# A fused attention and FFN block on one core: the first and the last unit worked by batches, one rope product, a shared set-up, and new orders at both ends

## The chip, the cores and the metric

The kernel runs on one core of one Trainium2 chip. The metric is the device time in microseconds of one launch. Lower is better.

## The reference

The input `x` is 32 sequences of 256 positions of 128 features, all float32. What is computed:

```
h = layernorm(x)
q, k, v, g = h @ Wq.T, h @ Wk.T, h @ Wv.T, h @ Wg.T      # 8 heads of 16
q, k = rope(q), rope(k)                                  # x * cos + rotate_half(x) * sin
kv, ksum, vsum = sum_s k^T v, sum_s k, sum_s v           # linear attention, no softmax
o = (q @ kv * scale + vsum) / (q @ ksum * scale + 256)
o = (o + conv5(v, lepe_w) + lepe_b) * g                  # depthwise, 5 taps along the sequence
x = x + o @ Wo.T
y = fp8(layernorm(x) as bf16 / s_in) @ fp8(W / s_k) * (s_in * s_k)
out = x + bf16(y) + bias
```

`fp8` rounds to e4m3fn.

## The kernel before

A unit is two batches (sequences), which is four tiles of 128 positions, so there are 16 units, `u` from 0 to 15 (`LAST`). Nearly all instructions take a whole unit: 128 partitions by 512 columns. `j` is a batch within its unit. All products run on TensorE into seven banks of PSUM. `p_num` takes two of them, and `bank[0]` to `bank[5]` are the rest.

There is no scheduler. Each of the five engines has one list of steps, written out by hand as calls such as `project_qk(2, 1)`, and it runs them in just that order. Each step waits on semaphores that count finished units (`count(u)` is unit `u`'s count). The units overlap as a software pipeline: while unit t has its first layernorm, unit t-1 has its projections, unit t-2 its attention, unit t-3 its output projection, unit t-4 its FFN. A loop over t covers the middle, and the first units and the last ones are written out.

The way of one unit, step by step:

- `stats1` (VectorE, L680), `var_eps1` (ScalarE), `pow1` (GpSimd, L476: the variance to the power -0.5, and then a small product, L478), `norm1` (ScalarE, L264), `transpose_h` (TensorE, L902), `move_hT` (ScalarE, L275);
- `project_qk` (TensorE, L912, one call for each batch), `rope` (VectorE, two products for each batch, L687 and L689), `add_rope` (GpSimd, L494, the sum of the two), `transpose_q` (L946) and `key_value` (L957) on TensorE, `mask_kv` (VectorE);
- `project_v` (L923), `transpose_v` (L938), and the five taps of the convolution: three on VectorE (`conv_tap`, L703), two on ScalarE, one sum on GpSimd (`sum_outer`);
- `sum_v` (L968) and `attend` (L976) on TensorE, `invert` and `divide` (VectorE, L727), `transpose_t1` (TensorE, L984), `add_lepe` and `gate` (VectorE, L735 and L743; `project_g`, L931, gives the gate), `project_o` (L991), `residual` (VectorE, L749);
- `stats2`, `var_eps2`, `pow2` (L485), `norm2`, `transpose_h2` (L1000), a quantising step (ScalarE, L358), `ffn` (TensorE, L1034), `move_y`, `add_bias`, `final_sum`, `store`.

For unit 15 the FFN part is already worked by batches (`end_norm2`, `end_transpose_h2`, `end_quantise`, `end_ffn`, `end_half`). Everything ahead of it is worked by whole units.

Before the first unit, TensorE transposes all five weight matrices once all of them and the identity are there, VectorE copies them out of PSUM, and `set_up_ffn` on VectorE rounds the FFN weights in 14 small instructions (L597 to L615 and L603), after a conversion of the identity to bf16 (L596). The loads of `x`, of the tables and of the outputs go through SyncE's queue (SP), four of the weights through ScalarE's. Loads of unit 2 and later stand behind all loads of constants on SP.

## Time and profile before

| | us |
|---|---|
| median of 3 runs | 181.34 (181.03 to 181.6) |
| the profiled execution | 181.48 |
| its span, first to last instruction | 179.7 |
| TensorE busy in the span | 160.3 (89%) |
| VectorE busy | 153.7 (86%) |
| GpSimd busy | 132.7 (74%) |
| ScalarE busy | 131.7 (73%) |

The profiled execution took 181.48 us, of which 1.8 us lie outside its span. Busy shares are averages over the whole span. In the middle all engines have more than these, and at both ends less, so each stage has to be read by itself. Durations of matmuls are modelled from their starts, and neighbours overlap a little. The distance from one start to the next is the better price.

### The profile page before, as it was taken

To read this page: it belongs to the slowest core of one execution; us is meant where nothing else is said; L and a number is where in the kernel's file an instruction comes from. 1 tells how busy PE (TensorE), PEld (TensorE's weight loads), DVE (VectorE), ACT (ScalarE), POOL (GpSimd) and SP (SyncE) were. 2 spreads that over 40 slices of the span, in tenths; PEclk is the share of its full clock that TensorE was granted. 3 is DMA by queue.
4 is the path that set the end of the run, shared out by engine and by line. 5 is a ranking of instruction groups with operands and counts; after the bars stand their busy time and mean duration, and the time that the engine had idled before them with its cause. 6 is when DMAs were issued, how large, how long until landed. Compare 5 with 4: busy or idle time off the path is not lost.

```text
span 179.7 us, 3861 instructions
## 1 busy us (share of the span) xinstructions
PE 160.3 (89%) x1125; PEld 138.4 (77%) x1125; DVE 153.7 (86%) x315; ACT 131.7 (73%) x353; POOL 132.7 (74%) x152
## 2 busy tenths in 40 slices
PE   0379979999999999999999999999999999998431
PEld 0258959878898889898989898989889888976210
DVE  0249999999999999999999999989999999999414
ACT  3443864879797979798888888887889586576561
POOL 1227155697989798888889898988899787838770
PEclk9999999999999999999999999999999999999955
DMA  5740000103012030304030303030301200200214
GB/s 144 207 117 0 0 0 7 58 0 92 28 44 74 21 101 3 115 4 119 4 117 0 117 7 117 4 117 0 104 15 57 67 4 1 58 5 0 62 55 117
DMA packets 19094, 9.71 MB, mean 54 GB/s; under 512 B 1536, under 2 KB 18816, under 8 KB 19072
## 3 DMA queue, kind: packets, MB, share of 16 engines
q1 hardware_dynamic: 18496, 9.19, 17.5%
q10 hardware_dynamic: 576, 0.26, 0.5%
q8 instruction: 10, 0.16, 0.4%
q14 instruction: 12, 0.10, 0.2%
HBM read 5.25 MB, written 4.19 MB: 53 GB/s over the span
## 4 chain that ended last, share of the span: by engine, by line
PE 81%; DVE 8%; issue 3%; ACT 3%; DMA 2%; POOL 1%; ACTq 0%; DVEq 0%; POOLq 0%
PE bank L912 16%; PE bank L991 8%; PE p_num L976 8%; PE bank L957 8%; PE p_num L968 8%; PE bank L923 7%; PE bank L931 7%; PE bank L946 4%; PE bank L902 4%; PE bank L984 4%; PE bank L938 4%; PE bank L1034 2%; DMA xs<-_attn_hidden_states_dram 2%; PE bank L1000 2%; DVE st L680 1%
## 5 line engine op out<-in xcount | busy, mean ns | idle before, releaser
L494 POOL TENSOR_TENSOR qk<-rc,rs 128x512 f32<-128x512 f32 x32 | 40.2, 1272 | 10.3 <-DVE rs L689 10.3
L912 PE MATMUL bank<-w_qk,hT 128*128 128x256 f32 x128 | 34.5, 397 | 0.9 <-ACT hT L275 0.9
L703 DVE SCALAR_TENSOR_TENSOR acc<-bank,conv_w,acc 128x510 f32<-128x510 f32 (+1 forms) x48 | 34.5, 719 | 0.1
L327 ACT ACTIVATE h<-x,nmr,rs 128x128 bf16<-128x128 f32 x60 | 24.7, 483 | 7.4 <-POOL nmr L487 7.4
L264 ACT ACTIVATE h<-xs,nmr,rs 128x128 f32<-128x128 f32 x64 | 26.2, 486 | 3.9 <-POOL nmr L478 3.9
L912 PEld LDWEIGHTS bank<-w_qk,hT 128*128 128x128 f32 x128 | 24.0, 199 | 4.8 <-ACT hT L275 1.3
L476 POOL TENSOR_TENSOR rs<-ve,minus_half 128x4 f32<-128x4 f32 x16 | 16.3, 1016 | 12.7 <-ACT ve L255 12.6
L485 POOL TENSOR_TENSOR rs<-ve,minus_half 128x4 f32<-128x4 f32 x16 | 16.3, 1017 | 11.1 <-ACT ve L318 11.0
L687 DVE TENSOR_TENSOR rc<-bank,cos_t 128x512 f32<-128x512 f32 x32 | 21.8, 681 | 3.0 <-PE bank L912 3.0
L505 POOL TENSOR_TENSOR acc<-acc,outer 128x508 f32<-128x508 f32 x16 | 20.3, 1267 | 2.3 <-DVE acc L703 2.3
L923 PEld LDWEIGHTS bank<-w_v,hT 128*128 128x128 f32 x128 | 17.6, 200 | 5.6 <-issue 5.3
L689 DVE TENSOR_TENSOR rs<-bank,sin_t 128x512 f32<-128x512 f32 x32 | 21.8, 681 | 0.0
L510 POOL TENSOR_TENSOR yc<-yb,fb 128x512 bf16<-128x512 bf16 x15 | 17.3, 1152 | 2.1 <-ACT yb L365 2.1
L680 DVE BATCH_NORM_STATS2 st<-xs 128x6 f32<-128x256 f32 x32 | 12.1, 419 | 7.7 <-DMA xs<-_attn_hidden_states_dram 7.7
L517 POOL TENSOR_TENSOR ob<-x,yc 128x512 f32<-128x512 f32 x15 | 17.3, 1156 | 1.2
L991 PE MATMUL bank<-w_o,oT 128*128 128x128 f32 x128 | 17.0, 276 | 1.0 <-DVE oT L743 0.9
L976 PE MATMUL p_num<-kvs,qT 128*128 128x136 f32 x128 | 17.9, 282 | 0.0
L358 ACT ACTIVATE q<-bank,rsc 128x512 fp8e4<-128x512 bf16 x15 | 10.3, 685 | 10.3 <-PE bank L1000 10.3
L923 PE MATMUL bank<-w_v,hT 128*128 128x128 f32 x128 | 17.7, 284 | 0.0
L957 PE MATMUL bank<-v,qk 128*128 128x136 f32 x128 | 17.7, 281 | 0.0
L968 PE MATMUL p_num<-w_v,hsum 128*128 128x272 f32 x64 | 17.3, 393 | 0.0
L991 PEld LDWEIGHTS bank<-w_o,oT 128*128 128x128 f32 x128 | 15.6, 192 | 2.0 <-DVE oT L743 2.0
(83 smaller groups left out, 335.6 us busy)
## 6 DMA issues: line engine op xcount, KB each, us to landing
xs<-_attn_hidden_states_dram SPq DMA_DIRECT2D x16, 256.0 KB, 2.9
out_dram<-ob SPq DMA_DIRECT2D x15, 256.0 KB, 2.6
cos_t<-in_cos_dram SPq DMA_DIRECT2D x1, 256.0 KB, 4.2
sin_t<-in_sin_dram SPq DMA_DIRECT2D x1, 256.0 KB, 4.9
out_dram<-ob SPq DMA_DIRECT2D x2, 128.0 KB, 1.8
mask<-in_mask_dram SPq DMA_DIRECT2D x1, 68.0 KB, 3.7
w_raw<-in_L_attn_Wq_dram ACTq DMA_DIRECT2D x1, 64.0 KB, 2.7
w_raw<-in_L_attn_Wk_dram ACTq DMA_DIRECT2D x1, 64.0 KB, 3.0
```

Source lines behind the costliest of these rows:

```text
L264: last = nc.scalar.activation(h[:, s, t], xs[:, u % NX, t], ACT.Identity, scale=rs1[:, s, t:t + 1], bias=nmr1[:, s, t:t + 1])
L327: last = nc.scalar.activation(h2[:, s, t], x2[:, u % 3, t], ACT.Identity, scale=rs2[:, s, t:t + 1], bias=nmr2[:, s, t:t + 1])
L494: nc.gpsimd.tensor_tensor(qk[:, u % 2, j].rearrange("p q t d -> p t q d"), rc[:, j].rearrange("p a h (q d) -> p (a h) q d", q=2), rs[:, j] ...
L687: nc.vector.tensor_tensor(rc[:, j], p_qk[j], cos_t[:].rearrange("p a (h d) -> p a h d", h=2), ALU.mult)
L689: nc.vector.tensor_tensor(rs[:, j], p_qk[j][:, :, ::-1, :], sin_t[:].rearrange("p a (h d) -> p a h d", h=2), ALU.mult).then_inc(rope_done[ ...
L703: nc.vector.scalar_tensor_tensor(out=part, in0=p_vT[:, :, lo + off:hi + off], scalar=conv_w[:, k:k + 1], in1=part, op0=ALU.mult, op1=ALU.a ...
L912: last = nc.tensor.matmul(p_qk[j][:, a].rearrange("p h d -> p (h d)"), hT[:, u % 3, t * P:(t + 1) * P], w_qk[:].rearrange("p a q d -> p (a ...
L923: last = nc.tensor.matmul(p_v[:, t], hT[:, u % 3, t * P:(t + 1) * P], w_v[:, 0:D], start=True, stop=True)
L957: last = nc.tensor.matmul(p_kv[:, t // TPB], qk_tile(u, 1, t), v[:, u % 3, t], start=(t % TPB == 0), stop=(t % TPB == TPB - 1))
L968: nc.tensor.matmul(p_num[:, TPB * j:TPB * (j + 1), 0:NW], hsum[:, u % 3, j:j + 1].to_broadcast([P, P]), w_v[:].unsqueeze(1).to_broadcast([ ...
L976: last = nc.tensor.matmul(p_num[:, t, 0:NW], qT[:, u % 2, t * P:(t + 1) * P], kvs[:, u % 2, t // TPB], start=False, stop=(t % TPB == TPB - 1))
L991: last = nc.tensor.matmul(p_proj[:, t], oT[:, u % 2, t * P:(t + 1) * P], w_o[:], start=True, stop=True)
```

## The change

Seven things are changed together.

1. The first unit's front (load, `stats1`, `var_eps1`, `pow1`, `norm1`, `transpose_h`, `move_hT`) goes by batches, into two banks.
2. The last unit's `attend`, `invert`, `divide`, `project_g`, `transpose_t1`, `add_lepe`, `gate`, `project_o`, `residual`, `stats2`, `var_eps2` and `pow2` go by batches, with banks of their own for each batch.
3. `rope` is one product of 1024 columns for each batch in place of two of 512: the result of `project_qk` is read twice against one table `turn`, which holds cos and sin. `add_rope` reads both halves of `turned`.
4. The set-up of the FFN is split: six small instructions stay on VectorE, the seven others run on GpSimd (`round_ffn_weights`). The identity is converted on ScalarE.
5. The weights of q and k are transposed apart from the other three, each set with a semaphore of its own. The constants' loads are split into two groups.
6. TensorE begins with 13 matmuls of zeros, 512 columns of bf16 each.
7. The lists of steps at both ends are in new orders (units 0 to 4 and 8 to 15).

```diff
@@ on SyncE
-            load_x(0)
-            sp.dma_start(ident[:], ident_c).then_inc(w_in, 16)
+            for j in range(BPU):
+                half = slice(TPB * j, TPB * (j + 1))
+                sp.dma_start(xs[:, 0, half], x_v[0][:, half]).then_inc(x_first[j], 16)
+            sp.dma_start(ident[:], ident_c).then_inc(wqk_in, 16)
+            sp.dma_start(turn[:], turn_c).then_inc(turn_in, 16)
             sp.dma_start(w_raw[:, 4], wo).then_inc(w_in, 16)
-            for dst, src in ((cos_t[:], cos_c), (sin_t[:], sin_c)):
-                sp.dma_start(dst, src).then_inc(rope_in, 16)
             load_x(1)
@@ on VectorE
-                nc.vector.tensor_tensor(rc[:, j], p_qk[j], cos_t[:].rearrange("p a (h d) -> p a h d", h=2),
-                                        ALU.mult)
-                nc.vector.tensor_tensor(rs[:, j], p_qk[j][:, :, ::-1, :],
-                                        sin_t[:].rearrange("p a (h d) -> p a h d", h=2),
-                                        ALU.mult).then_inc(rope_done[j], 1)
+                nc.vector.tensor_tensor(turned[:, j],
+                                        p_qk[j].rearrange("p a h d -> p a (h d)").unsqueeze(2).to_broadcast(
+                                            [P, TPB, 2, 2 * D]),
+                                        turn[:], ALU.mult).then_inc(rope_done[j], 1)
@@ on GpSimd, a new function
+            def round_ffn_weights():
+                val, e, r, n = (b[:, 0:D] for b in (qv, qe, qr, qn))
+                pool.wait_ge(scales_done, 1)
+                link(nc.gpsimd.tensor_scalar(e, e, 2.0 ** -6, 1.5 * 2.0 ** 20, ALU.max, ALU.mult))
+                link(nc.gpsimd.tensor_tensor(r, val, e, ALU.add))
+                link(nc.gpsimd.tensor_tensor(r, r, e, ALU.subtract))
+                link(nc.gpsimd.tensor_tensor(n, r, r, ALU.mult))
+                link(nc.gpsimd.tensor_scalar(n, n, 448.0 ** 2, 3e38, ALU.is_gt, ALU.mult))
+                link(nc.gpsimd.tensor_scalar(n, n, 3e38, 0.0, ALU.mult, ALU.mult))
+                nc.gpsimd.tensor_tensor(fwq[:], r, n, ALU.add).then_inc(w_ready, 1)
@@ on TensorE
+            def keep_busy(bank_free, times):
+                for _ in range(times):
+                    nc.tensor.matmul(bank_free[:], zero[:, 0:P], zero[:], start=True, stop=True)
...
-            transpose_h(0)
-            project_qk(0, 1)
+            pe.wait_ge(zero_set, 1)
+            keep_busy(p_gT, 13)
+            turn_weights_qk()
+            transpose_h(0, j=0)
+            turn_weights()
+            transpose_h(0, j=1)
```

The prediction speaks of three places in the orders. The first is the start of VectorE's list. `stats1` is `BN_STATS`, `rope` is the product with `rc`, `rs` or `turned`. Before:

```order
L680 BN_STATS st<-xs 128x6 x4
L588 COPY w_qk<-p_num 128x2x64 x2
L590 COPY w_v<-p_num 128x128
L591 COPY w_g<-p_num 128x128
L592 COPY w_o<-p_num 128x128
L687 TENSOR_TENSOR rc<-bank,cos_t 128x512
L689 TENSOR_TENSOR rs<-bank,sin_t 128x512
L687 TENSOR_TENSOR rc<-bank,cos_t 128x512
L689 TENSOR_TENSOR rs<-bank,sin_t 128x512
L680 BN_STATS st<-xs 128x6 x2
L596 CAST identb<-ident 128x128
```

And of the change, where the first `BN_STATS` row is unit 0 and the next two are units 1 and 2:

```order
L693 MEMSET zero 128x256
L803 BN_STATS st<-xs 128x6 x2
L699 COPY w_qk<-p_num 128x2x64 x2
L705 COPY w_v<-p_num 128x128
L709 COPY w_g<-p_num 128x128
L803 BN_STATS st<-xs 128x6 x2
L713 COPY w_o<-p_num 128x128
L803 BN_STATS st<-xs 128x6 x2
L812 TENSOR_TENSOR turned<-bank,turn 128x1024 x2
L717 RECIPROCAL rsc<-sc 128x2
L718 TENSOR_TENSOR ysc<-sc 128x1
```

`stats1(2)` has moved from behind the first unit's rope to ahead of it, and the cast is gone from this engine. The second place is TensorE's end, from `project_g(14)` on (L931 before). `ffn` stands twice in the program, under two branches, of which one runs. Before:

```order
L931 MATMUL bank<-hT,w_g 128x512
L976 MATMUL p_num<-kvs,qT 128x136 x4
L991 MATMUL bank<-w_o,oT 128x128 x4
L1000 MATMUL bank<-identb,h 128x128 x4
L984 MATMUL bank<-ident,t 128x128 x4
L1038 COMPARE_AND_BRANCH
L1034 MATMUL bank<-fwq,q 128x128 x4
```

Of the change, from `key_value(15)` on (L1187 is `attend(15)`, L1206 `project_o`, L1215 `transpose_h2`, L1141 `project_g(15)`):

```order
L1168 MATMUL bank<-v,qk 128x136 x4
L1157 MATMUL bank<-ident,qk 128x128 x4
L1206 MATMUL bank<-w_o,oT 128x128 x4
L1187 MATMUL p_num<-kvs,qT 128x136 x2
L1215 MATMUL bank<-identb,h 128x128 x4
L1187 MATMUL p_num<-kvs,qT 128x136 x2
```

These rows put `project_o(14)` ahead of `attend(15)`, which is cut in two around `transpose_h2(13)`. Then follow the branches of `ffn(13)`, and behind them TensorE's list goes on with unit 15 by batches, up to `transpose_h2(14)`:

```order
L1141 MATMUL bank<-hT,w_g 128x256 x2
L1196 MATMUL bank<-ident,t 128x128 x4
L1206 MATMUL bank<-w_o,oT 128x128 x4
L1215 MATMUL bank<-identb,h 128x128 x4
```

`project_g(15)` has moved ahead of `transpose_t1(15)`, which stood ahead of `ffn(13)` before. The third place is VectorE's end, from `residual(14)` on. Of the change (L889 is `stats2(14)`; the 16-column rows are `invert` of one batch, the 256-column rows `divide`, `add_lepe` and `gate` of one batch):

```order
L879 TENSOR_TENSOR x<-bank,xs 128x512
L844 TENSOR_SCALAR den<-p_num 128x16
L847 RECIPROCAL rden<-den 128x16
L889 BN_STATS st<-x 128x6 x2
L854 TENSOR_TENSOR t<-p_num,rden 128x256
L844 TENSOR_SCALAR den<-p_num 128x16
L847 RECIPROCAL rden<-den 128x16
L854 TENSOR_TENSOR t<-p_num,rden 128x256
L862 TENSOR_TENSOR t<-bank,acc 128x256
L871 TENSOR_TENSOR oT<-bank,t 128x256
L862 TENSOR_TENSOR t<-bank,acc 128x256
L871 TENSOR_TENSOR oT<-bank,t 128x256
```

Before, `invert(15)` and `divide(15)` stood ahead of `residual(14)`, and each step took the whole unit.

## Rows read from the trace of the kernel before

**Rows 1.** Stretches: us from:to, length, busy of each engine (instructions), clock, DMA.

```profile
10.00:15.00 5.00, 4.27 (x12) 3.55 (x13) 1.97 (x5) 2.60 (x10) 1.93 (x3) 1.00 0.26 77
...
45.00:145.00 100.00, 99.94 (x738) 88.86 (x737) 95.74 (x191) 83.90 (x228) 88.16 (x96) 1.00 0.19 55
...
165.00:170.00 5.00, 3.01 (x18) 1.72 (x18) 2.90 (x7) 2.65 (x8) 4.38 (x5) 1.00 0.18 52
170.00:175.00 5.00, 1.21 (x8) 0.69 (x8) 0.98 (x4) 3.12 (x8) 3.08 (x4) 0.50 0.18 52
```

**Rows 2.** The chain that ended last, in its middle: start us, us, what.

```profile
44.84 0.86 PE bank L931 x2
...
50.21 0.89 PE bank L991 x8
...
53.32 0.95 PE p_num L976 x8
...
129.91 0.86 PE bank L931 x2
```

**Rows 3.** Timeline of the start: start us, us, engine, line, what, count.

```profile
4.31 0.76 DVE L680 BATCH_NORM_STATS2 st<-xs 128x6 f32<-128x256 f32 x2 [4.31 <-DMA xs<-_attn_hidden_states_dram]
...
6.73 1.12 PE L887 MATMUL p_num<-ident,w_raw 128*128 128x128 f32 x4 [6.73 <-DMA w_raw<-in_L_attn_Wg_dram]
...
10.73 3.78 PE L912 MATMUL bank<-w_qk,hT 128*128 128x256 f32 x8 [0.93 <-ACT hT L275]
...
12.91 0.69 DVE L687 TENSOR_TENSOR rc<-bank,cos_t 128x512 f32<-128x512 f32 x1 [2.69 <-PE bank L912]
...
14.55 0.69 DVE L687 TENSOR_TENSOR rc<-bank,cos_t 128x512 f32<-128x512 f32 x1 [0.34 <-PE bank L912]
...
15.91 1.27 POOL L494 TENSOR_TENSOR qk<-rc,rs 128x512 f32<-128x512 f32 x1 [0.35 <-DVE rs L689]
...
26.12 0.66 PE L984 MATMUL bank<-ident,t 128*128 128x128 f32 x4 [0.49 <-DVE t L727]
```

**Rows 4.** DMA issues, x(2) in its window 7.0 to 7.3 us: KB, us to landing.

```profile
xs<-_attn_hidden_states_dram SPq DMA_DIRECT2D x1, 256.0 KB, 4.2
...
sin_t<-in_sin_dram SPq DMA_DIRECT2D x1, 256.0 KB, 4.9
...
out_dram<-ob SPq DMA_DIRECT2D x2, 128.0 KB, 1.8
```

**Rows 5.** Groups by line and shape: busy us, mean ns, idle before.

```profile
L687 DVE TENSOR_TENSOR rc<-bank,cos_t 128x512 f32<-128x512 f32 x32 | 21.8, 681 | 3.0 <-PE bank L912 3.0
L476 POOL TENSOR_TENSOR rs<-ve,minus_half 128x4 f32<-128x4 f32 x16 | 16.3, 1016 | 12.7 <-ACT ve L255 12.6
L727 DVE TENSOR_TENSOR t<-p_num,rden 128x512 f32<-128x512 f32 x16 | 10.9, 683 | 0.1
L478 POOL TENSOR_TENSOR nmr<-nm,rs 128x4 f32<-128x4 f32 x16 | 3.2, 199 | 1.3
L656 DVE TENSOR_TENSOR ob<-x,yc 128x256 f32<-128x256 f32 x2 | 0.8, 424 | 0.1
```

**Rows 6.** Timeline of VectorE's set-up for the FFN.

```profile
16.42 0.85 DVE L596 CAST identb<-ident 128x128 bf16<-128x128 f32 x1
...
18.41 0.23 DVE L609 TENSOR_SCALAR qe<-qe 128x128 f32<-128x128 f32 x1
...
20.50 0.15 DVE L603 COPY qe<-ysc 128x1 f32<-128x1 f32 x1
```

**Rows 7.** Timeline of the end.

```profile
160.52 0.39 PE L1034 MATMUL bank<-fwq,q 128*128 128x128 bf16 x4
...
166.90 0.69 DVE L743 TENSOR_TENSOR oT<-bank,t 128x512 f32<-128x512 f32 x1 [0.75 <-DVE t L735]
...
170.89 1.02 POOL L485 TENSOR_TENSOR rs<-ve,minus_half 128x4 f32<-128x4 f32 x1 [1.20 <-ACT ve L318]
...
176.97 0.42 DVE L656 TENSOR_TENSOR ob<-x,yc 128x256 f32<-128x256 f32 x1
```

More of the change, by code:

```diff
@@ L536, in _ @@
             pow2(1)
-            for t in range(6, 15):
+            for t in range(6, 13):
                 add_rope(t - 3, 1)
@@ L808, in _ @@
             conv_tap(3, 2)
-            for t in range(5, 14):
+            stats1(5)
+            add_lepe(2)
+            gate(2)
+            mask_kv(3)
+            rope(4, 1)
+            quantise_if_wide(1, is_small)
+            residual(2)
+            stats2(2)
+            conv_tap(4, 0)
+            rope(4, 0)
+            invert(3)
+            conv_tap(4, 1)
+            divide(3)
+            conv_tap(4, 2)
+            for t in range(6, 11):
                 stats1(t)
@@ L823, in _ @@
                 conv_tap(t - 1, 2)
+            stats1(11)
+            add_lepe(8)
+            gate(8)
+            rope(10, 1)
+            mask_kv(9)
+            quantise_if_wide(7, is_small)
+            residual(8)
+            stats2(8)
+            conv_tap(10, 0)
+            rope(10, 0)
+            invert(9)
+            conv_tap(10, 1)
+            divide(9)
+            stats1(12)
+            conv_tap(10, 2)
+            add_lepe(9)
+            gate(9)
+            mask_kv(10)
+            rope(11, 1)
@@ new lines, in _ @@
+            quantise_if_wide(8, is_small)
+            residual(9)
+            stats2(9)
+            rope(11, 0)
+            conv_tap(11, 0)
+            conv_tap(11, 1)
+            invert(10)
+            divide(10)
+            conv_tap(11, 2)
+            mask_kv(11)
+            stats1(13)
+            rope(12, 1)
+            add_lepe(10)
+            rope(12, 0)
+            gate(10)
+            quantise_if_wide(9, is_small)
+            invert(11)
+            residual(10)
+            divide(11)
@@ L861, in _ @@
+            stats2(13)
+            divide(14)
+            rope(15, 0)
+            add_lepe(14)
             conv_tap(15, 0)
-            stats2(13)
-            add_lepe(14)
+            gate(14)
             conv_tap(15, 1)
@@ new lines, in _ @@
+            project_g(9, (x2_done, count_last(8)))
+            project_v(11, (hT_done, count_first(11)))
+            project_qk(11, 1, (rope_done[1], count(10)))
+            transpose_t1(9, (qT_done, count(9)))
+            transpose_h2(8, (v_done, count(11)))
+            key_value(10, (rope_done[0], count(10)))
+            transpose_v(11, (tap_done[-1], count(10)))
+            ffn(8, is_small, (q8_done, count(8)))
+            transpose_q(10, (t2_done, count_last(9)))
+            project_o(9, (oT_done, count_last(9)))
@@ new lines, in _ @@
+            project_qk(11, 0, (kvs_done, count(10)))
+            sum_v(10, (t1_done, count_last(9)))
+            transpose_h(12, (yb_done, count(8)))
+            attend(10)
+            project_g(10, (x2_done, count_last(9)))
+            project_v(12, (hT_done, count_first(12)))
+            transpose_q(11, (qT_done, count(10)))
+            key_value(11, (rope_done[0], count(11)))
+            project_qk(12, 1, (rope_done[1], count(11)))
+            transpose_t1(10, (qT_done, count(11)))
@@ new lines, in _ @@
+            project_o(12, (oT_done, count_last(12)))
+            transpose_h2(11, (v_done, count(14)))
+            project_qk(14, 0, (kvs_done, count(13)))
+            sum_v(14, (t1_done, count_last(13)))
+            ffn(11, is_small, (q8_done, count(11)))
+            transpose_t1(13, (qT_done, count(13)))
+            project_g(13, (x2_done, count_last(12)))
+            transpose_h(15, (yb_done, count(11)))
+            key_value(14, (rope_done[0], count(14)))
+            transpose_q(14, (t2_done, count_last(13)))
@@ new lines, in _ @@
+            sum_v(15, (t1_done, count_last(14)))
+            key_value(15, (rope_done[0], count(15)))
+            transpose_q(15, (t2_done, count_last(14)))
+            project_o(14, (oT_done, count_last(14)))
+            attend(15, 0)
+            transpose_h2(13, (yb_done, count(12)))
+            attend(15, 1)
+            ffn(13, is_small, (q8_done, count(13)))
+            project_g(15, (tap_done[-1], count(15)), j=0)
+            project_g(15, (rope_done[1], count(15)), j=1)
+            transpose_t1(15, (qT_done, count(15)), j=0)
```

809 lines of the change are left out of this document (471 added, 338 removed).

## The prediction

> **What bounds the kernel now.** I read the stretches first, then the chain, then the timelines of the two ends. In the 100 us of the middle TensorE is busy 99.94 us, VectorE 95.74, GpSimd 88.16 and ScalarE 83.90, at a granted clock of 1.00 [rows 1]. The chain runs through TensorE's instructions back to back: one `project_g` starts at 44.84 and the one nine units later at 129.91 [rows 2], so a unit costs (129.91 - 44.84) / 9 = 9.45 us of TensorE, and nothing else matters there. The change takes no real product away from TensorE. So the middle keeps its length, unless another engine passes TensorE. Per unit VectorE has 95.74% x 9.45 = 9.05 us of work, 0.40 us under the bound.
>
> Sixteen units at 9.45 are 151 us of a span of 179.7. The other 28 to 29 us lie at the two ends, where TensorE waits or is slow, and there all of the change's effect must come from.
>
> The start: x is there at 4.31, the weights' transposes begin only at 6.73, `project_qk(0)` runs from 10.73 for 3.78 us, rope begins at 12.91, the second `add_rope` at 15.91, and the first `transpose_t1`, from which TensorE has hardly a gap, at 26.12 [rows 3]. The end: `ffn(12)` starts at 160.52 and is over at 160.91. From there to the last output sum (176.97 + 0.42 = 177.39) are 16.5 us, and 2.3 more to the end of the span [rows 7]. In this stretch TensorE is busy only 3.01 and 1.21 of 5 us [rows 1]: it is a chain of one unit through all engines.
>
> **The start after the change.** Two things limit it, one after the other.
>
> First, rope. It needs `project_qk(0)`, which comes earlier: the first batch's statistics can begin somewhat before 4.31, its power is small, and the two batches follow each other on GpSimd (1.02 + 0.20 us each [rows 5]). I get both halves of hT at about 9.3 instead of 10.7. With TensorE's clock up the first projections are done by about 10.8. But in the new order `stats1(2)` stands ahead of rope on VectorE. x(2) is still the 14th load on SP, is issued at 7.1 and lands 4.2 us later, at 11.3 [rows 4]. Two statistics take 0.76 [rows 3], so rope starts at 12.1, not at 10.8. That is 0.8 before the old 12.91. What the batches and the early clock win ahead of rope is mostly eaten by this wait: they are priced at nothing beyond the 0.8, with this load as their cover. If x(2) landed 1 us sooner, 1 us more would come.
>
> Second, from rope to the first `divide` VectorE is without a real pause, so its own work counts:
> - Rounding on GpSimd: the steps from 18.41 to the end of the copy (20.65) leave VectorE, 2.2 us [rows 6].
> - The cast leaves it: 0.85, some 0.8 net of the overlap with its neighbour [rows 6].
> - `stats1(2)` lies ahead of rope: 0.7 net. The wait of 0.34 between the two batches' ropes [rows 3] goes, since both projections are done.
> - Three merged products. A row of 256 columns costs 424 ns and one of 512 some 681 to 683 [rows 5], a slope of 1.0 ns per column, so 1024 columns cost about 0.68 + 0.52 = 1.20 us. Two old products take 1.36 as rows and 1.27 with their overlap; I take 0.07 saved for each rope, 0.2 in all. That the bank is read twice with stride 0 should cost nothing: `divide` reads `rden` with stride 0 and takes 683 ns like the others [rows 5].
>
> Sum: 0.8 + 2.2 + 0.8 + 0.7 + 0.3 + 0.2 = 5.0. TensorE has its own list to get through before `transpose_t1(0)` (attend, v, q and k, two transposes behind `mask_kv(0)`), which by the prices of [rows 2] ends 0.4 later than VectorE's (21.6 against 21.2). So TensorE reaches its saturated state **4.6 us** earlier. From there both engines have the same work as before, so the lead stays. Bounds: 3.3 (x(2) or the other constants 1 us later, as `sin_t` with its 4.9 us [rows 4] shows is possible) and 5.5.
>
> Rounding on GpSimd is seven operations of 128 columns behind `add_rope(1,0)`. The trace has none of that shape: between 0.20 (4 columns) and 1.27 (512 columns) [rows 3, 5], by columns 0.4 each, 2.8 to 3.5 us with the links. What is queued behind is `sum_outer(1)`, which needs the third tap of unit 1, not ready before some 27.4. The rounding starts at about 24. So it is covered up to about 0.5 us each. At 1.27 each it would end at 33 and hold up `add_rope(2)` and `key_value(2)` by some 3.5 us.
>
> The Trainium skill's page GPSIMD Engine Reference (3.1 Elementwise) speaks against this step: it measures a two-input operation on GpSimd at 1.96 times VectorE's, and keeps such work on VectorE. By that an operation would cost an estimated 0.57 us and the seven 4.0, which would cost the sum about 0.5 us; no row of the trace has this pair of operations to test it.
>
> The zeros: `project_qk(0)`'s eight instructions of 256 columns took 3.78, 0.47 each, where a middle one of 512 columns takes 0.43 [rows 2, 3]. So TensorE ran at half speed or less (1.2 GHz) after its first weights, though the stretch shows 1.00 [rows 1]. Thirteen instructions of 512 columns at half speed are 13 x 0.43 = 5.6 us, from about 1 to at most 6.6, when the first h arrives: they delay nothing.
>
> **The end after the change.** I count from the end of `ffn(12)`. TensorE does g(14), o(14), attend(15) and h2T(13): 0.86 + 0.89 + 0.95 + 0.2 = 2.9 [rows 2], with the first half of `attend(15)` over at 2.2. VectorE, after `residual(14)`, starts `invert(15,0)` at 2.5. A half product costs 0.42, net 0.35 [rows 5]. So: invert 2.9, stats2(14) 3.6, divide, invert, divide 4.7, then add_lepe and gate of both batches 6.2. `project_o(15,0)` lies beside the second batch. residual and stats2 of the first are done at 7.0, of the second at 7.8. Then power and small product on GpSimd. The power of four columns costs 1.02, and 0.82 of it is more than the plain product of the same shape [rows 5]; of two columns it costs between 0.6 (by columns) and 1.02; I take 0.8. `pow2(15,0)` starts at 7.6, behind `add_bias(13)` and `final_sum(13)`; the second's small product ends at 9.7, norm, transpose, quantising, product and the three last steps end at 13.1. Before, that point was 16.5. This is 3.4 us less, and I take 0.3 off for waits ahead of `attend(15)` such as the old list also had: **3.1 us**. Before, the gate of unit 15 stood at 6.0 (166.90) and the power at 10.0 (170.89) [rows 7]; the gain is made between these. Bounds: 0.5, if VectorE reaches `invert(15,0)` 2.5 us late, and 4.2, with the power at 0.6. Behind the last sum nothing changes: the store of 128 KB (1.8 us [rows 4]) stays.
>
> **Sum.** 4.6 + 3.1 = 7.7. The profiled execution would go from 181.48 to 173.8, and the median, 0.14 lower, from 181.34 to **173.6**.
>
> **Rivals.**
> - The clock falls again. The new start has pauses of TensorE of 1 to 2 us (ahead of `transpose_h(1)` and `transpose_q(0)`), and at the end the clock did fall to 0.50 once TensorE was busy 1.2 of 5 us [rows 1]. If it is down from 11 to 16, some 4.5 us of products between rope and `attend(0)` take twice as long, of which 2.7 are in the pauses anyway: +1.7, 175.3. For it: TensorE had worked with pauses from 6.73 on and was still slow in the 3.78 us from 10.73 [rows 3]. Against: 13 instructions without a gap. The Trainium skill's page TensorE: Matmul & The Clock Gate (Part 1) says that the clock is throttled by default, is released by sustained activity, and returns after idleness. By its rule the zeros do their work only if no long pause follows.
> - The end doesn't shorten: VectorE is late, because four other steps share its queue, and halves only pay fixed costs twice. Tail gain gone: 176.7. For it: VectorE is 95.7% full in the middle and has little with which to catch up [rows 1].
> - Rounding on GpSimd at 1.27 each: 177.1.
> - The new lists don't fill: a new order of units 8 to 15 loses in waits on TensorE what the ends give. 181.3. Against: TensorE is the bound with all others 4% or more below.
> - Slower: the merged rope is dear. With 0.40 us of slack per unit and two ropes in it, VectorE becomes the bound when one costs over 1.20 + 0.20 = 1.40 us. Over 13 units it eats 7.7 us at 1.40 + 7.7 / 26 = 1.70. If reading the bank twice with a table beside it went at half the rate for half the columns, 1.9 us, the time would be 173.6 + 26 x 0.5 = 186.6. Only the stride-0 row speaks on this, and against it.
> - More than forecast: x(2) early and the power at 0.6: below 172.
>
> **How the numbers follow.** Forecast 173.6 (its own range 172.0 to 175.0) 0.58; clock 0.10; end not shorter 0.13; GpSimd 0.04; more 0.07; nothing 0.03; slower 0.05. The first five are faster by over 0.3%, which is about what a measurement can tell from no change: 0.92. Same 0.03, slower 0.05. The range from 172.0 to 177.5 takes in the clock, the end, GpSimd, and leaves out 0.15 to 0.2.
>
> **What would show each step.** Right: rope of unit 0 starts at about 12.1, right behind the statistics of unit 2; `turned` at 1.20 us; the first `transpose_t1` at about 21.5; middle periods of 9.45; the seven rounding operations at 0.3 to 0.5, and no wait of `sum_outer(1)` for them; from the end of `ffn(12)` to the last sum near 13.1 us, where it was 16.5. Wrong: matmuls of the first projections still at 0.47, `turned` over 1.4, TensorE busy under 99% in the middle.

## The result and the profile after

The changed kernel takes **175.88 us** (median of 4 runs, 175.81 to 175.91), where the kernel before took 181.31 in the 4 runs beside it (181.03 to 181.6). The ratio is 0.970 (95% interval 0.9683 to 0.9717): 5.4 us or 3.0% faster. The forecast was 173.6 in a range of 172.0 to 177.5. The time lies in that range, but outside the 172.0 to 175.0 that belonged to the forecast itself. The gain came at the two ends, as predicted, and was 2.3 us smaller. The profiled execution took 175.88 us, with a span of 174.1 where the kernel before had 179.7.

The stretches of the changed kernel, with the columns of [rows 1]:

```profile
10.00:15.00 5.00, 4.04 (x21) 2.66 (x19) 3.96 (x9) 3.83 (x10) 3.27 (x4) 1.00 0.16 48
45.00:145.00 100.00, 99.80 (x733) 88.74 (x733) 94.53 (x168) 82.94 (x225) 86.10 (x93) 1.00 0.18 54
```

In the middle TensorE is as full as before (99.80 of 100 us). From 10 to 15 us VectorE has twice the work that it had [rows 1]: rope comes earlier.

The chain that ended last, read against [rows 2]:

```profile
7.07 3.88 DMA xs<-_attn_hidden_states_dram
11.73 2.25 DVE turned L812 x2
14.51 1.04 DVE qv L721
...
40.34 0.86 PE bank L1141 x2
50.05 0.86 PE bank L1141 x2
...
116.20 0.86 PE bank L1141 x2
...
157.86 0.89 PE bank L1206 x8
```

The chain begins with the load of x(2), and goes from there to rope. `project_g(2)` starts at 40.34 where it was 44.84 [rows 2], a lead of 4.5 us. `project_g(10)` starts at 116.20; before, it stood one unit of 9.45 ahead of the 129.91 of [rows 2], at 120.5, so the lead is 4.3 there. A middle unit still costs 9.45: (116.20 - 50.05) / 7. The step from `project_g(2)` to `project_g(3)` is 9.71, which is where a quarter of a microsecond is given back.

The timeline of the start, with the columns of [rows 3]:

```profile
1.18 4.98 PE L1083 MATMUL bank<-zero 128*128 128x512 bf16 x13 [1.18 <-DVE zero L693]
...
8.38 1.03 PE L1122 MATMUL bank<-w_qk,hT 128*128 128x256 f32 x4
...
10.14 1.03 PE L1122 MATMUL bank<-w_qk,hT 128*128 128x256 f32 x4
...
10.97 0.76 DVE L803 BATCH_NORM_STATS2 st<-xs 128x6 f32<-128x256 f32 x2 [1.26 <-DMA xs<-_attn_hidden_states_dram]
...
11.65 2.34 DVE L812 TENSOR_TENSOR turned<-bank,turn 128x1024 f32<-128x1024 f32 x2
...
12.94 2.52 POOL L583 TENSOR_TENSOR qk<-turned 128x512 f32<-128x512 f32 x2 [1.62 <-DVE turned L812]
...
14.43 1.11 DVE L721 TENSOR_SCALAR qv<-fw,rsc 128x128 f32<-128x128 bf16 x1
...
20.56 0.69 DVE L854 TENSOR_TENSOR t<-p_num,rden 128x512 f32<-128x512 f32 x1
...
22.14 0.60 PE L1196 MATMUL bank<-ident,t 128*128 128x128 f32 x4
...
24.12 0.65 POOL L570 TENSOR_SCALAR qe<-qe 128x128 f32<-128x128 f32 x1
...
28.16 1.27 POOL L595 TENSOR_TENSOR acc<-acc,outer 128x508 f32<-128x508 f32 x1 [0.19 <-DVE acc L827]
```

Four instructions of `project_qk(0)` take 1.03 us where eight took 3.78 [rows 3]. The projections of both batches are over at about 11.2. VectorE waited 1.26 us for x(2) with the statistics that stand ahead of rope. `transpose_t1(0)`, 26.12 before [rows 3], is at 22.14. Rounding on GpSimd runs from 24.12 to 27.98, and the `sum_outer` behind it waited 0.19 us, for VectorE's tap and not for the rounding. One step of VectorE's set-up, L721, took 1.11 us. In the timeline of the kernel before, the same step is:

```profile
17.83 0.29 DVE L601 TENSOR_SCALAR qv<-fw,rsc 128x128 f32<-128x128 bf16 x1
```

The timeline of the end, which answers to [rows 7]:

```profile
159.40 0.16 DVE L844 TENSOR_SCALAR den<-p_num 128x16 f32<-128x16 f32 x1
...
161.04 1.10 PE L1141 MATMUL bank<-hT,w_g 128*128 128x256 f32 x4
...
162.40 0.42 DVE L862 TENSOR_TENSOR t<-bank,acc 128x256 f32<-128x256 f32 x1 [0.79 <-PE bank L1196]
...
165.48 0.70 POOL L554 TENSOR_TENSOR rs<-ve,minus_half 128x2 f32<-128x2 f32 x1 [0.75 <-ACT ve L358]
...
169.25 1.15 POOL L609 TENSOR_TENSOR ob<-x,yc 128x512 f32<-128x512 f32 x1
169.61 0.94 DVE L772 TENSOR_TENSOR yc<-yb,fb 128x256 bf16<-128x256 bf16 x1
...
170.92 0.29 DVE L772 TENSOR_TENSOR yc<-yb,fb 128x256 bf16<-128x256 bf16 x1
171.24 0.42 DVE L776 TENSOR_TENSOR ob<-x,yc 128x256 f32<-128x256 f32 x1
```

The last sum ends at 171.66, before it was 177.39. The first batch's `add_lepe` (162.40) waited 0.79 us for its transposition on TensorE. One bias sum took 0.94 us and its twin 0.29.

To compare the tail at equal work: the kernel before had `project_g(14)` and `project_o(14)` still ahead of it at 160.91. The changed kernel stands there at 157.0 (before `project_o(14)`, 157.86, less the 0.86 of `project_g(14)`, which it has already done). The lead is 3.9 us. From there to the end of the last sum are 14.65 us, where it was 16.5.

### The profile page after: what moved, and what is told of

Its sections match the earlier page's. It is cut to its first block, busy times and chain, and to the rows that moved or that the text cites. A ratio compares the mean times of both kernels' runs of the same rounds, so it can differ in the third digit from the quotient of the medians.

```text
span 174.1 us, 3891 instructions
## 1 busy us (share of the span) xinstructions
PE 161.3 (93%) x1140; PEld 137.5 (79%) x1140; DVE 151.9 (87%) x281; ACT 132.5 (76%) x358; POOL 137.1 (79%) x163
## 2 busy tenths in 40 slices
DMA packets 18966, 9.71 MB, mean 56 GB/s; under 512 B 1536, under 2 KB 18816, under 8 KB 18944
## 4 chain that ended last, share of the span: by engine, by line
PE 83%; DVE 6%; SPq 3%; issue 2%; DMA 2%; POOL 1%; ACT 1%; DVEq 0%; ACTq 0%; POOLq 0%
PE bank L1122 14%; PE p_num L1187 9%; PE bank L1168 8%; PE bank L1206 8%; PE p_num L1179 8%; PE bank L1133 8%; PE bank L1141 8%; PE bank L1157 4%; PE bank L1196 4%; PE bank L1149 4%; PE bank L1112 4%; DMA xs<-_attn_hidden_states_dram 2%; PE bank L1249 2%; PE bank L1215 2%; DVE turned L812 1%
## 5 line engine op out<-in xcount | busy, mean ns | idle before, releaser
L583 POOL TENSOR_TENSOR qk<-turned 128x512 f32<-128x512 f32 x32 | 40.3, 1275 | 2.4 <-DVE turned L812 2.2
L812 DVE TENSOR_TENSOR turned<-bank,turn 128x1024 f32<-128x1024 f32 x32 | 38.6, 1215 | 0.7 <-PE bank L1122 0.3
L1122 PE MATMUL bank<-w_qk,hT 128*128 128x256 f32 x128 | 32.7, 380 | 0.0
L543 POOL TENSOR_TENSOR rs<-ve,minus_half 128x4 f32<-128x4 f32 (+1 forms) x17 | 16.6, 975 | 10.7 <-ACT ve L294 10.5
L1122 PEld LDWEIGHTS bank<-w_qk,hT 128*128 128x128 f32 x128 | 22.4, 191 | 2.4 <-issue 0.2
L554 POOL TENSOR_TENSOR rs<-ve,minus_half 128x4 f32<-128x4 f32 (+1 forms) x17 | 16.6, 977 | 8.5 <-ACT ve L358 8.5
L1133 PEld LDWEIGHTS bank<-w_v,hT 128*128 128x128 f32 x128 | 16.5, 192 | 5.0 <-issue 4.3
L1187 PE MATMUL p_num<-kvs,qT 128*128 128x136 f32 x128 | 18.2, 284 | 0.4 <-DVE kvs L838 0.4
L602 POOL TENSOR_TENSOR yc<-yb,fb 128x512 bf16<-128x512 bf16 x15 | 17.3, 1153 | 1.2 <-ACT yb L405 1.2
L1206 PE MATMUL bank<-w_o,oT 128*128 128x128 f32 x128 | 17.3, 277 | 0.8 <-DVE oT L871 0.8
L1133 PE MATMUL bank<-w_v,hT 128*128 128x128 f32 x128 | 16.9, 275 | 0.0
L1187 PEld LDWEIGHTS p_num<-kvs,qT 128*128 128x128 f32 x128 | 16.1, 190 | 0.9 <-issue 0.8
L1206 PEld LDWEIGHTS bank<-w_o,oT 128*128 128x128 f32 x128 | 15.7, 192 | 1.3 <-DVE oT L871 1.3
L1141 PE MATMUL bank<-hT,w_g 128*128 128x512 f32 (+1 forms) x34 | 16.4, 570 | 0.0
```

Of the source, the lines that this page charges most:

```text
L583: nc.gpsimd.tensor_tensor(qk[:, u % 2, j].rearrange("p q t d -> p t q d"), turned[:, j, :, :, 0:D].rearrange("p a h (q d) -> p (a h) q d", ...
L812: nc.vector.tensor_tensor(turned[:, j], p_qk[j].rearrange("p a h d -> p a (h d)").unsqueeze(2).to_broadcast([P, TPB, 2, 2 * D]), turn[:], ...
L1122: last = nc.tensor.matmul(p_qk[j][:, a].rearrange("p h d -> p (h d)"), hT[:, u % 3, t * P:(t + 1) * P], w_qk[:].rearrange("p a q d -> p (a ...
L1133: last = nc.tensor.matmul(p_v[:, t], hT[:, u % 3, t * P:(t + 1) * P], w_v[:, 0:D], start=True, stop=True)
L1141: nc.tensor.matmul(p_gT[:] if j is None else p_end_gT[j], w_g[:], hT[:, u % 3, part_of(j)], start=True, stop=True).then_inc(gT_filled, 1)
L1187: last = nc.tensor.matmul(p_num[:, t, 0:NW], qT[:, u % 2, t * P:(t + 1) * P], kvs[:, u % 2, t // TPB], start=False, stop=(t % TPB == TPB - 1))
```

## The experiments

Theory A, from the forecast: the front gains by what comes ahead of rope and by what leaves VectorE between rope and `divide(0)`; the end gains by the batches; its missing part lies in waits of the new end. The rivals are that another engine's order sets the start, so that x(2) is not the limit it seems, and that the new orders themselves cost time. Each run is a change to the changed kernel, except where it says otherwise. Ratios are to the kernel before, with their 95% intervals.

**e_cold: without the zeros.**

```diff
-            keep_busy(p_gT, 13)
```

> The changed kernel without the 13 matmuls of zeros; nothing else differs. The forecast's own price for a slow clock at the start is +1.7 us over the changed kernel's 175.88, so about 177.6, with project_qk(0) at 0.47 us an instruction and the first transpose_t1 near 23.8 instead of 22.14. Rival: what TensorE does before the first rope is covered by the wait for x(2), since rope starts only at 11.65 and both projections are done at 11.0. Then only what lies between rope and attend(0) can count, much of it in pauses, and the loss is 0.5 us or less (176.4).

176.83 us (175.94 to 177.68), ratio 0.9737 [0.9708, 0.9765]. The profiled execution was the slowest, 177.68. Its timeline of TensorE and VectorE:

```profile
9.55 1.91 PE L1122 MATMUL bank<-w_qk,hT 128*128 128x256 f32 x4
...
12.96 1.16 PE L1122 MATMUL bank<-w_qk,hT 128*128 128x256 f32 x4
...
14.16 1.23 DVE L812 TENSOR_TENSOR turned<-bank,turn 128x1024 f32<-128x1024 f32 x1 [1.11 <-PE bank L1122]
...
15.49 1.25 DVE L718 TENSOR_TENSOR ysc<-sc 128x1 f32<-128x1 f32 x1
```

The first four take 1.91 us and the last four 1.16, where the changed kernel has 1.03 for each four: by these durations TensorE runs at about half speed (1.2 of 2.4 GHz) up to about 13, though the granted clock of the stretch from 10 to 15 us reads 1.00. The second batch's rope now waits for TensorE. In this execution the zeros are worth 1.8 us, in the median 0.9, which lies between the two prices that were expected. Without the zeros the four runs lie within 1.7 us, with them within 0.1. But the changed kernel, run again later, had one run of 176.99 among five (the other four at most 175.96), so whether the zeros also make the time steadier is not shown.

**e_rope_first: `stats1(2)` behind the first unit's rope on VectorE.**

```diff
-            stats1(2)
             rope(0, 0)
             rope(0, 1)
+            stats1(2)
```

> The changed kernel with stats1(2) behind both ropes of unit 0 on VectorE, as it stood before. Theory A, the load of x(2) alone holds the start: rope starts at about 9.7 instead of 11.65 and the whole start moves by 1.5 us, to about 174.4. Theory B: ScalarE is the next bound, because norm1(1) and both taps of unit 0 stand there behind var_eps1(2), which now comes 1 us later (at about 12.8 instead of 11.8). Then conv_tap(0,0) starts at 16.3 or later where it started at 16.39, and the time stays within 0.5 us of 175.88, or is up to 1 us longer.

175.84 us (175.48 to 176.27), ratio 0.9694 [0.9669, 0.9719]: no difference from the changed kernel. Its timeline:

```profile
9.91 1.22 DVE L812 TENSOR_TENSOR turned<-bank,turn 128x1024 f32<-128x1024 f32 x1
...
16.63 1.53 DVE L827 SCALAR_TENSOR_TENSOR acc<-bank,conv_w,acc 128x510 f32<-128x510 f32 x2 [1.17 <-ACT acc L342]
```

Rope starts 1.7 us sooner, and nothing comes of it: VectorE then waits 1.17 us for ScalarE. ScalarE's list has `var_eps1(2)` ahead of `norm1(1)`, so the late x(2) now holds up ScalarE. The wait for x(2) was not removed but handed on.

**e_rope_norm_first: the same, and `norm1(1)` ahead of `var_eps1(2)` on ScalarE.**

```diff
-            var_eps1(2)
             norm1(1)
+            var_eps1(2)
```

> The same, and norm1(1) ahead of var_eps1(2) on ScalarE. By theory B the start now moves: norm1(1) begins at 11.4, the taps' inputs are there at 14.9, conv_tap(0,0) at 14.9, attend(0) at 16.8 instead of 18.40, and the time is about 174.4. If it stays at 175.9, something else holds attend(0).

174.68 us (174.46 to 175.42), ratio 0.9641 [0.9611, 0.967]. The timeline:

```profile
11.57 1.65 ACT L303 ACTIVATE h<-xs,nmr,rs 128x128 f32<-128x128 f32 x4 [0.41 <-POOL nmr L546]
...
21.07 0.60 PE L1196 MATMUL bank<-ident,t 128*128 128x128 f32 x4
```

`norm1(1)` runs 2.2 us sooner than in e_rope_first (13.73), `transpose_t1(0)` is at 21.07 where it was 22.14, and the time falls by 1.2. `attend(0)` is at 17.33 where the changed kernel has 18.40, and the chain that ended last no longer passes through x(2). So having steps that need x(2) ahead of steps that don't, in two queues at once, cost the changed kernel 1.1 to 1.2 us. Of the two moves only the first was run alone, and it gained nothing.

**e_round_on_dve: the rounding of the FFN weights back on VectorE.** Its seven steps and the copy behind them stand behind the first ropes again, and GpSimd has none.

```diff
-                nc.vector.tensor_scalar(qe[:, 0:D].bitcast(I32), qv[:, 0:D].bitcast(I32), 0x7F800000, None,
-                                        ALU.bitwise_and).then_inc(scales_done, 1)
+                round_e4m3fn(fwq[:], D, lambda n, ins: link(ins))
+                nc.vector.tensor_copy(qe[:, 0:1], ysc[:]).then_inc(w_ready, 1)
@@ on GpSimd
-            round_ffn_weights()
```

> The changed kernel with the rounding of the FFN weights back on VectorE, in the same place of its list. The forecast's price is 2.2 us of VectorE between rope(0) and the first divide. If VectorE's list sets the lead at the start, the time goes to 177.5 to 178.1. If TensorE's list sets it (the first transpose_t1 stood 0.9 us behind VectorE's divide), some 0.9 of it is free and the time is about 177.1. If the lead is set elsewhere, it stays at 175.9.

179.0 us (178.25 to 179.75), ratio 0.9886 [0.9843, 0.993]. Two of its four executions took 178.25 and 178.27, the other two 179.72 and 179.75. The profiled one took 178.25 with a span of 176.5. Its timeline of TensorE:

```profile
20.72 1.17 PE L1186 MATMUL p_num<-kvs,qT 128*128 128x136 f32 x8 [2.72 <-DVE kvs L837]
...
24.45 0.60 PE L1195 MATMUL bank<-ident,t 128*128 128x128 f32 x4
```

`transpose_t1(0)` is 2.3 us later (22.14 before), and the span 2.4 longer. That is the forecast's 2.2 for this part. The 1.5 us more of the other two executions have no trace, and stay unexplained. Of the pieces of the front that were tested, this was the largest. On GpSimd nothing waited for it.

**e_two_products: rope as two products of 512 columns each.**

```diff
-                nc.vector.tensor_tensor(turned[:, j],
-                                        p_qk[j].rearrange("p a h d -> p a (h d)").unsqueeze(2).to_broadcast(
-                                            [P, TPB, 2, 2 * D]),
-                                        turn[:], ALU.mult).then_inc(rope_done[j], 1)
+                for n in range(2):
+                    last = nc.vector.tensor_tensor(turned[:, j, :, n], p_qk[j].rearrange("p a h d -> p a (h d)"),
+                                                   turn[:, :, n], ALU.mult)
+                last.then_inc(rope_done[j], 1)
```

> The changed kernel with rope as two products of 512 columns again, on the same tables and tiles. The forecast's price is 0.07 us of VectorE for each rope. In the middle it is covered by TensorE; at both ends VectorE sets the pace over some 10 ropes: +0.2 to +0.7 us, 176.1 to 176.6. If VectorE's slack of the middle is worth more than that, nothing: 175.9. More than 1 us would mean that VectorE bounds the middle.

176.61 us (176.43 to 177.52), ratio 0.9746 [0.9722, 0.977]: 0.7 slower. The merged product in the changed kernel's groups by shape, with the columns of [rows 5]:

```profile
L812 DVE TENSOR_TENSOR turned<-bank,turn 128x1024 f32<-128x1024 f32 x32 | 38.6, 1215 | 0.7 <-PE bank L1122 0.3
```

And the products of this kernel, in the same view:

```profile
L813 DVE TENSOR_TENSOR turned<-bank,turn 128x512 f32<-128x512 f32 x64 | 40.7, 681 | 0.6 <-PE bank L1122 0.4
```

1215 ns against 2 x 681, which overlap: the first unit's two ropes take 2.47 us here and 2.34 merged, so a merged rope saves 0.07, as forecast, and the stride-0 read of the bank shows no cost. In the middle this is slack of VectorE. At the start `transpose_t1(0)` comes 0.36 later (22.50 instead of 22.14), more than the 0.13 of two ropes. The timeline of VectorE shows the rest:

```profile
14.29 1.23 DVE L719 TENSOR_TENSOR qr<-rsc 128x1 f32<-128x1 f32 x1
```

This product of one column lasts until 15.52, just behind GpSimd's second `add_rope` (15.50). L721 takes 0.28 here but comes behind it, and ends at 15.91, where it ended at 15.54. So most of the 0.36 is a wait that fell on another step. The other 0.3 of the 0.7 was not traced.

**e_last_whole: unit 15 worked as a whole again, in the new orders.** The calls with `15, 0` and `15, 1` from `attend` to `pow2` become one call each.

```diff
-            invert(15, 0)
+            invert(15)
             stats2(14)
-            divide(15, 0)
-            invert(15, 1)
-            divide(15, 1)
-            add_lepe(15, 0)
-            gate(15, 0)
-            add_lepe(15, 1)
-            gate(15, 1)
+            divide(15)
+            add_lepe(15)
+            gate(15)
```

> The changed kernel with unit 15 worked as a whole from attend to pow2, in the same places of the lists. If the batches make the gain at the end, the chain from attend(15) (over at 160.0) to the last sum (171.66) grows by 1.2 to 1.8 us, and the time is 177.1 to 177.7. If the end was shortened by the new order alone and halves pay their fixed costs twice for nothing, it stays within 0.5 us of 175.88.

178.61 us (178.52 to 178.67), ratio 0.9844 [0.9824, 0.9864]: 2.7 slower, more than either number expected. The timeline of the end:

```profile
163.10 0.69 DVE L860 TENSOR_TENSOR t<-bank,acc 128x512 f32<-128x512 f32 x1 [1.53 <-PE bank L1188]
...
167.82 1.01 POOL L553 TENSOR_TENSOR rs<-ve,minus_half 128x4 f32<-128x4 f32 x1 [2.71 <-ACT ve L358]
```

`pow2(15)` is 2.3 us later than the first of the two in the changed kernel. So within these orders the batches are worth 2.7. That is more than the whole tail won (1.85), so the new orders without the batches must lose.

**e_front_only: the new front up to unit 4, and from there the old orders, unit 15 whole.** This separates the front from the rest.

```diff
@@ VectorE, and likewise on the three other engines
-            stats1(5)
...
-            for t in range(6, 11):
+            for t in range(5, 14):
```

> The changed kernel's front (batches of unit 0, zeros, split set-up, merged rope, the new orders up to unit 4) with the old orders from there on, and unit 15 worked as a whole. By the positions of project_g in the chains the front is worth 4.25 us, so 177.1 if the rest is as before. The new end in itself (new order and batches) is then worth 1.2 to 1.5. Rival: new late orders help even without batches; then this one is at 178.6 or above, where the new order with a whole unit 15 stood.

177.04 us (176.75 to 178.23), ratio 0.9776 [0.9752, 0.9799]. The front alone gives 4.3 us. The late orders without batches cost 1.6 (178.61 against 177.04), the batches give 2.7, and the net of the end is 1.1 to 1.2. Its chain, at `project_g(14)`:

```profile
156.49 0.91 PE bank L1041 x2
```

That is 4.4 us ahead of the kernel before (160.91), while the changed kernel leads by 3.9 at this point of the work. e_last_whole leads by as much, since its `project_o(14)` starts at 157.71 in the timeline and the changed kernel's at 157.70. So about 0.5 of the 1.6 is lost in the lists ahead of this point. Behind it e_last_whole needs 17.3 us to the end of the last output sum (174.31) and e_front_only 16.4 (172.89). Of these 0.9 us, 0.8 is a bias sum that took 1.10 in e_last_whole, beside a sum of GpSimd, and 0.29 in e_front_only. The changed kernel, run again beside this one, took 175.96 (175.87 to 176.99, ratio 0.9717 [0.9694, 0.974]):

> The changed kernel itself again, as the reference of this group: 175.9 us, ratio 0.970.

**e_t1_early: each batch's `transpose_t1(15)` ahead of its `project_g(15)` on TensorE.**

```diff
-            project_g(15, (tap_done[-1], count(15)), j=0)
-            project_g(15, (rope_done[1], count(15)), j=1)
             transpose_t1(15, (qT_done, count(15)), j=0)
+            project_g(15, (tap_done[-1], count(15)), j=0)
             transpose_t1(15, (x2_done, count_last(14)), j=1)
+            project_g(15, (rope_done[1], count(15)), j=1)
```

> The changed kernel with transpose_t1(15,0) ahead of project_g(15,0), and transpose_t1(15,1) ahead of project_g(15,1). Theory: add_lepe(15,0) starts 0.8 us late because its transpose stands behind both gates' products. Then add_lepe(15,0) starts at about 161.65 instead of 162.40 and the time is 0.6 to 0.75 us shorter, 175.2. Rival: the end is held by GpSimd's and ScalarE's work for units 13 and 14 (final_sum(13) ends at 164.74, shortly before the first power at 165.48), so the lead is given back there and less than 0.3 us is left.

175.15 us (175.04 to 175.27), ratio 0.9652 [0.9635, 0.967]: 0.7 faster. The timeline:

```profile
161.68 0.41 DVE L862 TENSOR_TENSOR t<-bank,acc 128x256 f32<-128x256 f32 x1
...
164.84 0.70 POOL L554 TENSOR_TENSOR rs<-ve,minus_half 128x2 f32<-128x2 f32 x1
```

`add_lepe(15,0)` comes 0.7 sooner (162.40 in the changed kernel) and all behind it moves with it. The transposition had stood behind two products that nothing on the path needed yet.

**e_bias_f32 and e_bias_psum: the 0.94 us bias sum.** It runs while GpSimd does `final_sum(14)` (169.25 to 170.40), and ends 0.15 behind it. Either its types were slow (bf16 against bf16, with a table read by stride 0), or it waited for GpSimd. The first kernel reads the bias from a float32 copy, the second from a bank of PSUM; each copy is made on ScalarE ahead of the sums.

```diff
+            nc.scalar.activation(fb32[:], fb[:], ACT.Copy).then_inc(fb32_set, 1)
...
-                nc.vector.tensor_tensor(yc[:, s, half], yb[:, s, half], fb[:].unsqueeze(1).to_broadcast([P, TPB, D]),
+                nc.vector.tensor_tensor(yc[:, s, half], yb[:, s, half], fb32[:].unsqueeze(1).to_broadcast([P, TPB, D]),
```

> The changed kernel, in which the bias that VectorE adds for unit 15 is a float32 copy (same values), made on ScalarE at the start. In the changed kernel the first of these sums of bf16 by bf16 took 0.94 us while GpSimd ran a sum, and the second 0.29 with GpSimd idle. Theory: an operation of VectorE of the fast kind waits for GpSimd's running operation to end, one with a float32 operand doesn't. Then both take about 0.42, the last sum ends 0.4 to 0.5 us earlier, and the time is 175.4. Rival: the first sum was long for its own reasons (its input from PSUM just written, its first use of the bias); then it stays at 0.9 or more and the time at 175.9 or above.

176.44 us (176.32 to 177.86), ratio 0.974 [0.9712, 0.9768]: not better. The timeline of its two sums:

```profile
169.58 1.15 POOL L613 TENSOR_TENSOR ob<-x,yc 128x512 f32<-128x512 f32 x1
169.85 1.16 DVE L777 TENSOR_TENSOR yc<-yb,fb 128x256 bf16<-128x256 bf16 x1
...
171.39 0.42 DVE L777 TENSOR_TENSOR yc<-yb,fb 128x256 bf16<-128x256 bf16 x1
```

The first takes 1.16 and again ends behind GpSimd's end (170.73). The second takes 0.42, where the bf16 table gave 0.29. The types were not the cause of the long sum, and the expectation that a float32 operand would end the wait was wrong.

```diff
+            nc.scalar.activation(p_num[:, 0, 0:D], fb[:], ACT.Copy).then_inc(fbp_set, 1)
...
+                nc.vector.tensor_tensor(yc[:, s, half], yb[:, s, half], p_num[:, 0:1, 0:D].to_broadcast([P, TPB, D]),
```

> The changed kernel, in which the bias of unit 15's two sums is read from PSUM (ScalarE copies it there after var_eps2(15,1)). The float32 copy in SBUF left the first sum as long as it was (1.16 us). Theory now: what waits for GpSimd's running sum is an operation of VectorE with two inputs in SBUF, whatever their type. Then the first sum takes 0.45 us or less beside GpSimd's final_sum(14), and the wait moves on to the next operation with two inputs in SBUF, the first output sum, which ends about 0.15 to 0.4 us behind GpSimd's. The time gains 0.1 to 0.4 us at most, or loses ScalarE's copy, 0.2. Rival: the sum was long for another reason than its second input's place; then it stays at 0.9 or more.

176.01 us (175.93 to 176.04), ratio 0.9707 [0.9694, 0.972]: the same time. But the timeline tells the two theories apart:

```profile
169.33 1.15 POOL L612 TENSOR_TENSOR ob<-x,yc 128x512 f32<-128x512 f32 x1
169.69 0.42 DVE L776 TENSOR_TENSOR yc<-yb,p_num 128x256 bf16<-128x256 bf16 x1
170.15 0.62 DVE L780 TENSOR_TENSOR ob<-x,yc 128x256 f32<-128x256 f32 x1
```

With one input in PSUM the bias sum runs through beside GpSimd in 0.42 us. The next sum, which has two inputs in SBUF, now takes 0.62 instead of 0.42 and ends at 170.77, 0.29 behind GpSimd's 170.48. The wait is for GpSimd's running instruction, and it moves to the next that reads two inputs from SBUF. The second bias sum takes 0.41 here instead of 0.29 and the last sum ends at 171.55 instead of 171.66, so the time gains nothing that can be seen. In e_front_only, where GpSimd was done by 170.90, both bias sums (from 171.48 on) took 0.29 and 0.28.

**e_both_ends: the moves of e_rope_norm_first and e_t1_early together.**

> The changed kernel with three moves: stats1(2) behind both ropes of unit 0 and norm1(1) ahead of var_eps1(2) (alone 173.1 us of span against 174.1), and transpose_t1 of unit 15 ahead of project_g (alone 173.4). If the two ends are independent of each other, the gains add up: span near 172.3, time 174.0 to 174.2. If the lead at the start is given back at the end, it stays at 174.7 or above.

**174.15 us** (173.93 to 174.85), ratio 0.9614 [0.9595, 0.9633], which beats both kernels: 1.7 us below the changed one, 1.8 below its second run. The gains nearly add up (1.2 + 0.7 = 1.9), as was expected if the two ends are independent: one lies ahead of the saturated middle and the other behind it.

## Why the prediction was right, and where its size was off

- **TensorE bounds the middle, and the middle stays.** Right: 9.45 us for a unit, TensorE 99.80% busy. All of the gain came from the two ends.
- **Start, first limit: rope waits for x(2).** Right in its mechanism: rope at 11.65 (forecast 12.1), right behind the statistics of unit 2, because the load took 3.88 us and not 4.2 [rows 4]. The sentence "If x(2) landed 1 us sooner, 1 us more would come" was not worked out for ScalarE: e_rope_first shows that taking away VectorE's wait alone was worth nothing, and e_rope_norm_first that taking it away in both queues gives 1.1 to 1.2 us. An earlier load itself was tried in no run.
- **Start, second limit: VectorE's work from rope to the first `divide`.** Right in most of its terms: the divide leads by 4.8 us where the sum was 5.0, the 2.2 for the rounding measured 2.3 (e_round_on_dve), the merged products cost 1.215 where 1.20 was taken. The term that failed is the 0.8 for the cast. From the start of the cast to the end of L601 the kernel before took 1.70 us (16.42 to 18.12). The changed kernel, which has no cast there, took 1.63 for the same steps (13.91 to 15.54), because L721, 0.29 before, took 1.11: it ran beside GpSimd's second `add_rope` and ended just behind it (15.46). Before, it was the cast that ended just behind an `add_rope`. So taking the cast away won 0.1 and not 0.8, and the earlier rope gave 0.4 back.
- **Where that limit ends.** Not at the `divide`. The chain leaves VectorE at `mask_kv(0)` (17.82). From `attend(0)` to `transpose_t1(0)` TensorE then has its own list, 18.40 to 22.14, and these 3.7 us are the same in the trace of every experiment. So `transpose_t1(0)` stands 0.9 behind the end of the divide, where 0.4 was forecast. TensorE led by 4.0 there, by 4.5 at `project_g(2)` and by 4.2 to 4.3 from unit 3 on, where 4.6 was forecast. e_front_only gives 4.3 in the time.
- **Rounding on GpSimd.** Its size was a little low (3.9 us in all, forecast 2.8 to 3.5), its cover right: nothing behind it waited for it. The estimate that the prediction made from the Trainium skill's page GPSIMD Engine Reference (3.1 Elementwise), 4.0 for all seven, came out by luck: a two-input sum took 0.46 against VectorE's 0.29, 1.6 times and not 1.96, while the two operations with a comparison or a maximum took 0.65 against 0.23.
- **The zeros.** Right, and with them the first rival (the clock falls again) fell: four instructions of 256 columns took 1.03 us, and those of the same shape behind the pauses up to 22 us took 1.03 again. The rival's price of 1.7 was close for the execution in which it did happen (e_cold, 1.8).
- **The end: 3.1 forecast, 1.85 measured by equal work, 1.1 to 1.2 in the time.** This is the term that was mis-sized. `invert(15,0)` came as forecast (2.5 us behind the common point: 159.40 - 157.0 = 2.4). Then: `add_lepe(15,0)` was taken to follow `divide` at 4.7, but came at 162.40 - 157.0 = 5.4, because `transpose_t1` stood behind the two `project_g(15)` on TensorE: 0.7 (e_t1_early gives just that back). The rows of the order printed ahead of the prediction show that place, and the sum had no term for it. And the bias sum waited 0.65 for GpSimd, 0.94 instead of 0.29. The two powers were taken as 0.8 and took 0.70, a little better. The two waits are 1.35 of the 1.55 us by which the tail was longer than 13.1. The first is confirmed by a run. The second is read from the trace alone, since in e_bias_psum it only moved on. In the rest, TensorE's clock may have a part: the granted clock from 165 to 170 us was 0.57, where it was 1.00 before [rows 1], after TensorE had been busy 3.53 and 2.23 us of two stretches of 5. Two transpositions there took 0.40 us, and 0.28 in e_bias_f32, where the clock of the stretch was 0.87.
- **The lists between.** From `project_g(10)` to the common point the lead fell by 0.35 (4.3, then 3.9), about the 0.3 that the forecast took off for waits there. With the old late orders it rose instead, from 4.1 to 4.4 (e_front_only). So the new lists ahead of the end lose 0.5; which wait takes it stays open. e_last_whole and e_front_only show that the new late orders cost 1.6 in all when unit 15 is whole. The forecast had "a new order of units 8 to 15 loses in waits" among its rivals, as an all-or-nothing case. It is real, in part.
- **Sum.** 4.3 + 1.1 = 5.4, forecast 4.6 + 3.1 = 7.7. The rival "the end does not shorten" (176.7) was half true: VectorE was not late, but TensorE's order and GpSimd were. The rivals of a dear rope and of a dear rounding fell. That 175.9 still lies in the range up to 177.5 is in part luck: the room above 175.0 was left for a slow clock, an end without gain and a dear rounding, and the first and the last did not come.

## What to carry to other kernels

When a late load holds up one engine's list, look for every list in which a step that needs it stands ahead of a step that doesn't: moving it in VectorE's list alone gave 0.0 us, in VectorE's and ScalarE's 1.2. Splitting the last unit into batches pays more in an order in which each batch's next step comes first on every engine (one transposition moved ahead gave 0.7 us), so walk the path engine by engine and give a term to each instruction that stands ahead without being needed. And when a step is dear in a trace, ask whether it worked or waited for another engine before its time is booked as a gain: the cast of 0.85 us was taken away, and a step priced at 0.29 by its old row took 1.11 in its place.
